# A transformer layer on one core: a new order of stores, bias additions, transposes and feed-forward turns

## The chip, the cores and the metric

The kernel runs on one core of a Trainium2 chip. The metric is the device time of one execution, in microseconds. A core has five engines that run their own instruction streams and meet at semaphores: TensorE (PE, matrix products; PEld is its loading of weights), VectorE (DVE), ScalarE (ACT), GpSimd (POOL) and SyncE (SP), which here issues all DMAs. Products land in PSUM, everything else lies in SBUF.

## The reference

The input x has 16 batches of 1024 rows of 256 numbers. The layer is, cut to what matters:

```python
xn = layernorm(x)
Q, K, V = xn @ Wq.T + bq, xn @ Wk.T + bk, xn @ Wv.T + bv       # 16 heads of 16
Q, K = rope(Q), rope(K)
weights = softmax(where(causal, Q @ K.T / 4, -1e9))
attn = (weights @ V) @ Wo.T + bo
y = square(relu(xn @ W_fc.T)) @ W_proj.T                        # 256 -> 1024 -> 256
spikes = count over 5 steps of a leaky threshold driven by y    # a step function of y
out = x + attn + spikes / 5
```

As the spikes are a step function of y, the kernel computes y nearly exactly: every operand of the projections is split into a high and a low part (xT_hi and xT_lo, h_hi and h_lo, and the weights), and three products are summed for each.

## The kernel before

The work is a pipeline over batches. `interval(b, ...)` exists once for each engine and lays the attention of batch b beside the preparation of batch b + 1 (its transposes, projections, rotation and the feed-forward part). There are 17 of them: one ahead (b = -1, no attention), one for b = 0, a loop for b = 1 to 13, one for b = 14, and a last one (b = 15, with the second half of its own feed-forward part and no projection).

An interval has 18 steps of 5 places, written (step, place). The places 0, 1, 3 and 4 hold one score group each: scores of 2 heads for 512 queries in all, against one to two tiles of 128 keys, in one of two PSUM buffers (`scores`, L1353), which ScalarE turns into probs (`weigh`, L759). TensorE waits before a group until the exponential of the group two before it is done. Place 2 holds a run of products of probs with v (`weigh`, L1370) and, for the batch before, `output`. Everything else stands in tables that map a place to work, and each engine walks its own part of them in this order. So an instruction that waits holds back all that stands behind it on its engine. GpSimd masks the tiles on the diagonal (L665), and the runs of products wait for these masks.

The parts that the change touches:

- Transposes of xn (`T_AT`, L1133) at place 2 of steps 2 and 3, split by ScalarE (`high_xT`, L716) and VectorE (`low_xT`, L865).
- Projection and rotation of four units u = 0 to 3 (`QK_AT`, L1153; `rotate`, L884 to L891): VectorE writes rot (eo = 0) and rot_b (eo = 1). GpSimd adds them (`sum_qk`, L647), ScalarE takes the high part into planes (`plane_qk`, L722), VectorE writes the low part over rot_b (`low_qk`, L895), and SyncE stores both to qk_dram (`store_planes`, L424). There are two buffers of each, so unit u waits for what unit u - 2 left: the second half of rotate, for the landing of its store (`planes_out[u % 2]`). The next projection waits for the rotation (`rot_done`), and so does the first expansion.
- The ring: SyncE reads q and k of a quad of heads (four in a batch) back into one of two slots with 13 DMAs (`load_ring`, L433 and L436), once the scores of the quad two before are done.
- The feed-forward part is cut in turns of 24 products (`MLP_AT`, L1175 and L1184). An item of it takes ScalarE's relu, VectorE's square and cast, and GpSimd's difference h_lo (L657). `Y_AT` is where VectorE takes a finished y.
- `add_bias` (L642) adds the output bias to rs, the residual rows, on GpSimd.

In the lines that stand below, `att` says that there is attention, `last` that there is a batch before it, `more` that there is one after.

## Time and profile before

| | us |
|---|---|
| median of 3 runs | 2242.65 (2242.55 to 2243.33) |
| the profiled execution | 2242.55 |
| its span, first to last instruction | 2240.8 |
| busy: TensorE | 2128.1 (95%) |
| busy: ScalarE | 1454.4 (65%) |
| busy: VectorE | 1385.8 (62%) |
| busy: GpSimd | 1112.1 (50%) |
| mean granted clock of TensorE | 0.988 |

The page gives for each group of instructions its busy time, the mean of one, and what ended the idle time before it. TensorE's share is above all others. In the 40 slices of the span it is at nine tenths or more in all but the first three and the last one, and the granted clock is at nine tenths or more in all but the second and the last. 46.6% of the time of the 16 DMA engines is taken by SyncE's queue. The timeline gives the start, length and idle time before each instruction, in us from the span's start.

### The profile page before, as it was taken

The page shows a single profiled execution, that of the slowest core. Times are in us where ns is not written, and L with a number is a line of the kernel's source. Part 1 is how long each engine was busy: PE and PEld are TensorE (multiplying, and loading weights), DVE is VectorE, ACT ScalarE, POOL GpSimd, SP SyncE. Part 2 cuts the span into 40 slices and gives each one's busy share as a digit, 9 for nine tenths or more (in the row PEclk, how much of TensorE's full clock was granted, in tenths as well). Part 3 has the DMA queues.
Part 4 walks back from the last instruction along what each step waited for, and adds up shares of the span by engine and source line. Part 5 has one row for each costly group of instructions (what it writes and reads, how often), then busy time and mean ns, then how long its engine had stood idle before and what let it go on. Part 6 is the DMA issues. An engine that isn't in the chain of part 4 may idle for free.

```text
span 2240.8 us, 67671 instructions
## 1 busy us (share of the span) xinstructions
PE 2128.1 (95%) x25492; PEld 1516.1 (68%) x25492; DVE 1385.8 (62%) x2134; ACT 1454.4 (65%) x1673; POOL 1112.1 (50%) x1074
## 2 busy tenths in 40 slices
PE   3789999999999999999999999999999999999995
PEld 2657677676767767676776767677676776767653
DVE  5555565675767657566665756667575666757543
ACT  2276766667676666767666676666767666676662
POOL 3445454463645547354553735455364544646341
PEclk9899999999999999999999999999999999999998
DMA  3354453535455363544536455453644535364442
GB/s 122 111 157 112 129 162 93 181 107 167 117 134 168 88 196 102 155 133 118 180 88 189 117 139 150 104 180 99 179 114 136 162 94 183 108 167 118 115 111 69
DMA packets 169850, 299.97 MB, mean 134 GB/s; under 512 B 25088, under 2 KB 114944, under 8 KB 157184
## 3 DMA queue, kind: packets, MB, share of 16 engines
q1 hardware_dynamic: 169600, 296.10, 46.6%
q8 instruction: 222, 3.64, 0.7%
q14 instruction: 28, 0.23, 0.0%
HBM read 174.89 MB, written 103.28 MB: 124 GB/s over the span
## 4 chain that ended last, share of the span: by engine, by line
PE 74%; DMA 6%; issue 6%; POOL 5%; DVE 4%; ACT 2%; SPq 0%; POOLq 0%; DVEq 0%; ACTq 0%
PE pair L1175 20%; PE pair L1370 18%; PE pair L1353 11%; PE pair L1184 10%; PE pair L1153 7%; PE pair L1115 6%; DMA recip_rows<-recip_dram 5%; POOL probs L665 3%; PE pair L1167 2%; ACT probs L759 2%; POOL h_lo L657 1%; POOL rs L642 1%; DMA recip_dram<-denom 1%; PE pair L1308 1%; DVE rot_b L891 1%
## 5 line engine op out<-in xcount | busy, mean ns | idle before, releaser
L759 ACT ACTIVATE probs<-pair 128x1024 f32<-128x1024 f32 x1152 | 1149.7, 1027 | 457.5 <-PE pair L1353 456.2
L657 POOL TENSOR_TENSOR h_lo<-h_sq,h_hi 128x512 fp32r<-128x512 f32 x256 | 386.7, 1510 | 467.7 <-DVE h_hi L963 467.4
L1184 PE MATMUL pair<-wproj_hi,h_hi 64*128 64x256 f32 x2048 | 599.1, 293 | 0.1
L1175 PE MATMUL pair<-xT_hi,wfc_hi 64*128 64x256 f32 x2048 | 556.2, 291 | 20.3 <-POOL h_lo L657 6.8
L1184 PE MATMUL pair<-wproj_hi,h_lo 64*128 64x256 f32 x2048 | 572.9, 280 | 0.0
L1184 PE MATMUL pair<-wproj_lo,h_hi 64*128 64x256 f32 x2048 | 572.1, 279 | 0.0
L665 POOL TENSOR_SCALAR_AFFINE_SELECT probs<-probs 128x512 f32<-128x512 f32 x512 | 386.4, 772 | 367.4 <-ACT probs L759 366.5
L1370 PE MATMUL pair<-probs,v_sb 128*17 128x512 f32 (+3 forms) x6144 | 549.9, 489 | 7.5 <-POOL probs L665 6.6
L1175 PE MATMUL pair<-xT_lo,wfc_hi 64*128 64x256 f32 x2048 | 536.8, 280 | 0.0
L1175 PE MATMUL pair<-xT_hi,wfc_lo 64*128 64x256 f32 x2048 | 536.0, 280 | 0.0
L1353 PE MATMUL pair<-q_ring,k_ring 64*128 64x512 f32 (+3 forms) x3072 | 463.3, 355 | 14.0 <-ACT probs L759 12.8
L1175 PEld LDWEIGHTS pair<-xT_hi,wfc_hi 64*128 64x128 f32 x2048 | 358.0, 187 | 72.2 <-PE pair L1175 31.4
L1184 PEld LDWEIGHTS pair<-wproj_lo,h_hi 64*128 64x128 f32 x2048 | 383.5, 187 | 1.8
L1184 PEld LDWEIGHTS pair<-wproj_hi,h_lo 64*128 64x128 f32 x2048 | 383.2, 187 | 0.0
L1184 PEld LDWEIGHTS pair<-wproj_hi,h_hi 64*128 64x128 f32 x2048 | 381.6, 186 | 0.9 <-issue 0.3
L961 DVE TENSOR_TENSOR h_sq<-h_sq 128x512 f32<-128x512 f32 x256 | 196.2, 766 | 292.7 <-ACT h_sq L751 289.5
L1353 PEld LDWEIGHTS pair<-q_ring,k_ring 64*128 64x128 f32 x3072 | 263.1, 186 | 160.7 <-ACT probs L759 89.0
L1175 PEld LDWEIGHTS pair<-xT_hi,wfc_lo 64*128 64x128 f32 x2048 | 359.5, 188 | 3.1
L1175 PEld LDWEIGHTS pair<-xT_lo,wfc_hi 64*128 64x128 f32 x2048 | 359.5, 188 | 0.0
L1370 PEld LDWEIGHTS pair<-probs,v_sb 128*17 128x17 f32 x6144 | 151.0, 97 | 281.6 <-issue 236.9
L751 ACT ACTIVATE h_sq<-pair 128x512 f32<-128x512 f32 x256 | 153.5, 600 | 179.5 <-PE pair L1175 101.1
L975 DVE SCALAR_TENSOR_TENSOR count<-y_sb,count 128x512 bf16<-128x512 f32 x256 | 261.5, 1022 | 4.2
(89 smaller groups left out, 2907.0 us busy)
## 6 DMA issues: line engine op xcount, KB each, us to landing
q_ring<-qk_dram SPq DMA_DIRECT2D x384, 128.0 KB
k_ring<-qk_dram SPq DMA_DIRECT2D x384, 128.0 KB
qk_dram<-planes SPq DMA_DIRECT2D x64, 512.0 KB, 2.8
qk_dram<-rot_b SPq DMA_DIRECT2D x64, 512.0 KB, 3.7
xn<-in_x SPq DMA_DIRECT2D x17, 1024.0 KB, 5.6
rs<-in_x SPq DMA_DIRECT2D x64, 256.0 KB, 2.8
acc_dram<-rs SPq DMA_DIRECT2D x64, 256.0 KB, 4.9
attn<-numer SPq DMA_DIRECT2D x256, 64.0 KB, 2.3
```

The source lines that it names most:

```text
L657: pool.tensor_tensor(h_lo[i % HB][:, :], h_sq[i % HB][:, :], h_hi[i % HB][:, :].bitcast(F32), ALU.subtract).then_inc(h_lo_done, 1)
L665: ins = pool.affine_select(view, view, [[0, 4], [1, P]], ALU.is_ge, 0.0, base=0, channel_multiplier=-1)
L751: act.activation(h_sq[i % HB][:, :], fc_bank[i % 2], ACT.Relu).then_inc(relu_done, 1)
L759: act.activation(probs[BUFFER[n]][:, 2 * pr:2 * pr + 2, :], pair[m % NSLOT][:, :, :], ACT.Exp, scale=SCALE).then_inc(exp_done, 1)
L961: dve.tensor_tensor(sq, sq, sq, ALU.mult).then_inc(sq_h, 1)
L975: dve.scalar_tensor_tensor(count[:, :], y, edges[s], count[:, :], ALU.is_gt, ALU.add).then_inc(spike_step, 1)
L1115: ins = pe.matmul(bank, lhsT, rhs, start=n == 0, stop=n == len(parts) - 1)
L1153: ins = pe.matmul(qk_bank[eo], w[rows, k, m], x[rows, k, cols], start=turn == 0 and n == 0, stop=turn == 1 and n == len(terms) - 1, skip_g ...
L1175: return pe.matmul(fc_bank[i % 2][:, a * T2:(a + 1) * T2], w[rows, k, m], x[rows, k, g * T2:(g + 1) * T2], start=turn == 0 and n == 0, sto ...
L1184: return pe.matmul(proj_bank[:, t * D:(t + 1) * D], h[rows, a * T2 + t * P:a * T2 + (t + 1) * P], w[rows, f, :], start=i % ITEMS_OF_GROUP ...
L1353: ins = pe.matmul(pair[m % NSLOT][:, half, to:to + width(kt, g)], k_ring[rows, slot, pr, kt * P:(kt + 1) * P], q_ring[rows, slot, pr, q0:( ...
L1370: ins = pe.matmul(pv_bank[32 * i:32 * i + VW, q0 - g * G:G], v_sb[:, kt, 4 * quad + i, :], probs[BUFFER[n]][:, i, at:at + width(kt, g)], s ...
```

## The change

It moves work and changes nothing of what is computed.

- SyncE: in the step 5 part, the load of the third quad's ring stands first, then for each unit the store of out and then that of the planes. Before, the planes stood ahead of out, and the ring behind the second of both.
- VectorE: `low_qk(u)` leaves the middle of the rotation of unit u + 1 and stands at place 3 of steps 4, 5 and 6; `low_xT` stands behind the copies of numer and the division.
- ScalarE: `plane_qk` is one place later, `high_xT` at place 2 and not 0.
- TensorE: the transposes stand behind the run of products; turns 2 to 16 and 22 to 24 of the feed-forward part stand at other places (most a place or two later).
- GpSimd: the four bias additions of a half stand together, at (2, 4) and at (13, 4). Before, they stood in pairs at (8, 2), (10, 2), (14, 2) and (15, 4).

```diff
--- before.py
+++ after.py
@@ -116,9 +116,9 @@
          (5, 4): (3, 0), (6, 0): (3, 1)}
 ROTATE_AT = {at: u for at, (u, turn) in QK_AT.items() if turn}
 SUM_QK_AT = {(3, 2): 0, (4, 2): 1, (5, 2): 2, (6, 2): 3}
-PLANE_AT = {(3, 4): 0, (4, 4): 1, (5, 4): 2, (6, 4): 3}
+PLANE_AT = {(4, 0): 0, (5, 0): 1, (6, 0): 2, (7, 0): 3}
 SQUARE_AT = {(4, 2): 0, (5, 2): 1, (6, 2): 2, (7, 2): 3}
-LOW_QK_AT = {(7, 2): 3}
+LOW_QK_AT = {(4, 3): 0, (5, 3): 1, (6, 3): 2, (7, 2): 3}
 O_AT = {4: 0, 5: 1, 6: 2, 7: 3}
 NORM_AT = 8
 NORM_PAIR = 4 * NORM_AT + 2
@@ -126,10 +126,10 @@
 
 
 
-MLP_AT = {(6, 4): (0,), (7, 0): (1,), (7, 4): (2,), (8, 0): (3,), (8, 2): (4, 5), (8, 4): (6,), (9, 0): (7,),
...
+MLP_AT = {(6, 4): (0,), (7, 0): (1,), (8, 0): (2,), (8, 2): (3, 4), (9, 0): (5,), (9, 3): (6,), (9, 4): (7,),
...
@@ -137,7 +137,7 @@
...
-Y_AT, Y_FIRST = {(10, 0): 0, (13, 0): 1, (16, 0): 2}, {(10, 1): 0, (13, 0): 1}
+Y_AT, Y_FIRST = {(10, 1): 0, (13, 0): 1, (16, 0): 2}, {(10, 1): 0, (13, 0): 1}
 Y_FINAL = {(11, 3): 2, (15, 3): 3}
 Y_CARRIED_AT = (1, 0)
...
@@ -182,7 +182,7 @@
 SPIKES_NEXT = {(14, 1): (0, 0), (14, 2): (0, 1), (14, 3): (0, 2), (14, 4): (0, 3), (15, 1): (0, 4), (15, 2): (0, 5),
                (15, 3): (1, 0), (15, 4): (1, 1), (16, 1): (1, 2), (16, 2): (1, 3), (16, 3): (1, 4), (17, 1): (1, 5)}
 SPIKES_FINAL = {(16, 0): 0, (17, 0): 1}
-BIAS_HERE_AT, BIAS_NEXT_AT = {(8, 2): (0,), (10, 2): (1,)}, {(14, 2): (0,), (15, 4): (1,)}
+BIAS_HERE_AT, BIAS_NEXT_AT = (2, 4), (13, 4)
 STATS_AT = {(10, 3): range(0, 4), (11, 4): range(4, 8)}
 VAR_AT, ROOT_AT = (11, 4), (12, 0)
 XN_AT, XN_FIRST = {(16, 4): range(0, 4), (17, 4): range(4, 8)}, {(13, 4): range(NT)}
@@ -530,12 +530,12 @@
                         load_ring(b, d, 1, b * 2 * NUNIT if last else None)
                     if last and n == 3:
                         load_fin(b - 1, d - 1, again)
+                    if att and n == 5:
+                        load_ring(b, d, 2, b * 2 * NUNIT + 2 * NU)
+                    if last and n in (5, 6, 7, 8):
+                        store_out(b - 1, d - 1, n - 5)
                     if more and n in (5, 6, 7, 8):
                         store_planes(nb, nd, n - 5)
-                    if last and n in (5, 6, 7, 8):
-                        store_out(b - 1, d - 1, n - 5)
-                    if att and n == 6:
-                        load_ring(b, d, 2, b * 2 * NUNIT + 2 * NU)
                     if att and n == 8:
                         gather(b, 0, last)
                     if norm and n == 8:
@@ -683,12 +683,14 @@
                         sum_qk(nb, SUM_QK_AT[at])
                     for i in expanded.get(at, ()) if more or final else ():
                         h_low(item, i)
-                    for a in BIAS_HERE_AT.get(at, ()) if att else ():
-                        add_bias(b, 1, a, again)
-                    for a in BIAS_NEXT_AT.get(at, ()) if more else ():
-                        if first and a == 0:
+                    if att and at == BIAS_HERE_AT:
+                        for a in range(2):
+                            add_bias(b, 1, a, again)
+                    if more and at == BIAS_NEXT_AT:
+                        if first:
                             pool.wait_ge(bias_done, 1)
-                        add_bias(nb, 0, a, again)
+                        for a in range(2):
+                            add_bias(nb, 0, a, again)
 
             root(0)
             low_weight(2)
@@ -776,7 +778,7 @@
                         weigh(b, 2 * n + place // 3, place % 3, last)
                     for m in take_v_at.get(at, ()) if att else ():
                         take_v(b, m)
-                    for m in T_AT.get(n, ()) if place == 0 and (more or final) else ():
+                    for m in T_AT.get(n, ()) if place == 2 and (more or final) else ():
                         high_xT(tb, m)
                     if more and at in PLANE_AT:
                         plane_qk(nb, PLANE_AT[at])
@@ -1010,23 +1012,20 @@
                         take_y(item + (y_at[at] + 1) * ITEMS_OF_GROUP, y_at[at])
                     if last and at == (0, 2):
                         take_numer(b - 1, *NUMER_AT[n], last)
-                    for m in T_AT.get(n, ()) if place == 2 and (more or final) else ():
-                        low_xT(tb, m)
                     if att and n and place == 2 and n in NUMER_AT:
                         take_numer(b, *NUMER_AT[n], last)
                     if last and at == INVERT_LAST:
                         invert(b - 1, 1)
                     if last and at == DIVIDE_LAST:
                         divide(b - 1, 1)
+                    for m in T_AT.get(n, ()) if place == 2 and (more or final) else ():
+                        low_xT(tb, m)
                     if more and at in ROTATE_AT:
-                        u = ROTATE_AT[at]
-                        if first and u == 0:
+                        if first and ROTATE_AT[at] == 0:
                             dve.wait_ge(table_in, 16)
                             dve.wait_ge(consts_done, 2)
-                        rotate(nb, u, 0, items_before(b, again) if att else None)
-                        if u:
-                            low_qk(nb, u - 1)
-                        rotate(nb, u, 1, None)
+                        for eo in range(2):
+                            rotate(nb, ROTATE_AT[at], eo, items_before(b, again) if att else None)
                     if last and place == 2 and n in O_AT:
                         finish(b - 1, O_AT[n])
                     if more and at in LOW_QK_AT:
@@ -1387,8 +1386,6 @@
                     n, place = at
                     if att and place != 2:
                         scores(b, 2 * n + place // 3, place % 3, last, more)
-                    for m in T_AT.get(n, ()) if place == 2 and (more or final) else ():
-                        transpose(b, tb, m, att, again)
                     if last and at == (0, 2):
                         run(b - 1, LAST_RUN, last)
                     if att and place == 2 and n in RUN_AT:
@@ -1397,6 +1394,8 @@
                         if att:
                             pe.wait_ge(exp_done, b * 2 * NUNIT + NORM_PAIR - NSLOT + 1)
                         norms(nb, first_norm_bank if first else norm_bank)
+                    for m in T_AT.get(n, ()) if place == 2 and (more or final) else ():
+                        transpose(b, tb, m, att, again)
                     if last and place == 2 and n in O_AT:
                         output(b - 1, O_AT[n])
                     if att and at in values_at:
```

SyncE in the loop, around the stores of unit 0 and the third ring (L424 is `store_planes`, L481 `store_out`, L433 and L436 `load_ring`). Before, from the store of rot_b of unit 0 to the first instruction of the ring load:

```order
L424 DMA qk_dram<-rot_b 128x2x512
L362 REGISTER_ALU
L481 DMA out<-fin 128x2x256
L362 REGISTER_ALU
L424 ISA
L424 DMA qk_dram<-planes 128x2x512
L424 ISA
L424 DMA qk_dram<-rot_b 128x2x512
L362 REGISTER_ALU
L481 DMA out<-fin 128x2x256
L362 REGISTER_ALU
L433 ISA
```

and now, from the last DMAs of the same ring load to the store of rot_b of unit 0:

```order
L433 DMA k_ring<-qk_dram 16x2048 x3
L436 ISA
L436 DMA q_ring<-shift_dram 2x2048
L362 REGISTER_ALU
L481 DMA out<-fin 128x2x256
L362 ISA
L424 ISA
L424 DMA qk_dram<-planes 128x2x512
L424 ISA
L424 DMA qk_dram<-rot_b 128x2x512
```

The 13 ring DMAs (q_ring, k_ring) moved from behind the second unit's stores to before those of the first, and out is ahead of the planes.

TensorE behind the last `output` (L1115, now L1114) in step 7, up to the first products of turn 2; the rows with q_ring are score groups. Before:

```order
L1115 MATMUL pair<-wo_sb,attn 128x256 x4
L1346 REGISTER_ALU
L1353 MATMUL pair<-q_ring,k_ring 128x512 x2
L1346 REGISTER_ALU
L1353 MATMUL pair<-q_ring,k_ring 128x512 x2
L1218 REGISTER_ALU
L1175 MATMUL pair<-xT_hi,wfc_hi 128x256
L1184 MATMUL pair<-wproj_hi,h_hi_53 128x256
```

and now:

```order
L1114 MATMUL pair<-wo_sb,attn 128x256 x4
L1345 REGISTER_ALU
L1352 MATMUL pair<-q_ring,k_ring 128x512 x2
L1345 REGISTER_ALU
L1352 MATMUL pair<-q_ring,k_ring 128x512 x2
L1345 REGISTER_ALU
L1352 MATMUL pair<-q_ring,k_ring 128x512 x2
L1217 REGISTER_ALU
L1174 MATMUL pair<-xT_hi,wfc_hi 128x256
L1183 MATMUL pair<-wproj_hi,h_hi_53 128x256
```

The group of (8, 0) has come before turn 2, so three groups follow one another.

GpSimd in steps 13 and 14, with h_lo of item 10 first (h_lo_59), the bias additions (rs) and the masks (probs). Before:

```order
L657 TENSOR_TENSOR h_lo_59<-h_sq_51,h_hi_55 128x512
L362 ISA
L665 AFFINE_SELECT probs<-probs 128x4x128 x2
L640 ISA
L642 TENSOR_TENSOR rs<-rs,bo_sb 128x256 x2
L656 REGISTER_ALU
L657 TENSOR_TENSOR h_lo_60<-h_sq_52,h_hi_56 128x512
L362 ISA
L665 AFFINE_SELECT probs<-probs 128x4x128 x2
```

and now:

```order
L657 TENSOR_TENSOR h_lo_59<-h_sq_51,h_hi_55 128x512
L640 ISA
L642 TENSOR_TENSOR rs<-rs,bo_sb 128x256 x4
L362 ISA
L665 AFFINE_SELECT probs<-probs 128x4x128 x2
L656 REGISTER_ALU
L657 TENSOR_TENSOR h_lo_60<-h_sq_52,h_hi_56 128x512
L362 ISA
L665 AFFINE_SELECT probs<-probs 128x4x128 x2
```

Four bias additions stand now before the masks of unit 28 and, behind h_lo of item 11, of unit 29; before there were two, between these masks.

## Rows read from the trace of the kernel before

**Rows 1.** Windows: one pass; columns in its heading.

```profile
core 0: us, PE busy (x) PEld busy (x) DVE busy (x) ACT busy (x) POOL busy (x), PEclk, DMA share, GB/s
1163.80:1296.20 132.40, 130.88 (x1596) 93.39 (x1594) 85.45 (x131) 90.33 (x105) 68.62 (x66) 1.00 0.48 138
```

**Rows 2.** Timeline (start, us, engine, line, out<-in, [idle before <-releaser]) of VectorE, numer.

```profile
1105.95 0.68 DVE L998 COPY numer<-pair 128x512 f32<-128x512 f32 x1
...
1238.36 0.68 DVE L998 COPY numer<-pair 128x512 f32<-128x512 f32 x1
```

**Rows 3.** Timeline of SyncE's queue, steps 4 to 6 of a pass.

```profile
1196.10 0.39 SPq L424 DMA_DIRECT2D qk_dram<-rot_b  x1
...
1205.80 0.65 SPq L481 DMA_DIRECT2D out<-fin  x1
...
1206.78 3.86 SPq L433 DMA_DIRECT2D q_ring<-qk_dram  x6
...
1216.30 0.38 SPq L424 DMA_DIRECT2D qk_dram<-rot_b  x1
```

**Rows 4.** Timeline of TensorE, the same steps.

```profile
1192.54 0.40 PE L1353 MATMUL pair<-q_ring,k_ring 64*128 64x512 f32 x2
...
1205.44 0.40 PE L1153 MATMUL pair<-xT_hi,wqk_hi 64*128 64x512 f32 x2
...
1213.63 0.28 PE L1175 MATMUL pair<-xT_hi,wfc_hi 64*128 64x256 f32 x2
...
1215.05 0.40 PE L1353 MATMUL pair<-q_ring,k_ring 64*128 64x384 f32 x4
```

**Rows 5.** Answer on the tile rot_b, one pass: issue to landing.

```profile
DMA to landing us min/median/max: 3.6/3.7/4.9
```

**Rows 6.** Timeline of VectorE, rotation of unit 2 in step 5.

```profile
1201.86 1.21 DVE L895 TENSOR_TENSOR rot_b<-rot,planes 128x1024 fp32r<-128x1024 f32 x1
1202.99 0.74 DVE L890 SCALAR_TENSOR_TENSOR rot_b<-pair,neg_bqk,table 128x512 f32<-128x512 f32 x1
```

**Rows 7.** Windows: two stretches of the last batch's attention.

```profile
2137.40:2140.80 3.40, 2.04 (x18) 1.03 (x20) 0.69 (x1) 2.59 (x3) 0.49 (x1) 1.00 0.70 198
2140.80:2144.20 3.40, 3.40 (x17) 0.50 (x9) 0.00 (x0) 1.18 (x2) 2.20 (x5) 0.50 0.24 82
```

**Rows 8.** Timeline of TensorE: a run of products at either clock.

```profile
1186.42 1.91 PE L1370 MATMUL pair<-probs,v_sb 128*17 128x512 f32 x16
...
2140.63 3.53 PE L1370 MATMUL pair<-probs,v_sb 128*17 128x512 f32 x16
```

**Rows 9.** Timeline of TensorE, steps 2 and 3 of a pass.

```profile
1179.39 2.35 PE L1370 MATMUL pair<-probs,v_sb 128*17 128x512 f32 x32
...
1189.36 0.50 PE L1153 MATMUL pair<-xT_hi,wqk_hi 64*128 64x512 f32 x2 [0.37 <-DVE rot_b L891]
```

**Rows 10.** Timeline of TensorE: score groups of the last stretch.

```profile
2146.05 0.73 PE L1353 MATMUL pair<-q_ring,k_ring 64*128 64x512 f32 x4
2147.72 0.49 PE L1353 MATMUL pair<-q_ring,k_ring 64*128 64x512 f32 x2 [0.94 <-ACT probs L759]
```

**Rows 11.** Timeline of GpSimd, steps 3 and 14.

```profile
1189.39 2.40 POOL L647 TENSOR_TENSOR rot<-rot,rot_b 128x1024 f32<-128x1024 f32 x1 [3.85 <-DVE rot_b L891]
...
1271.78 1.40 POOL L665 TENSOR_SCALAR_AFFINE_SELECT probs<-probs 128x512 f32<-128x512 f32 x2
...
1273.16 1.87 POOL L642 TENSOR_TENSOR rs<-rs,bo_sb 128x256 f32<-128x256 f32 x2
...
1276.12 1.67 POOL L657 TENSOR_TENSOR h_lo<-h_sq,h_hi 128x512 fp32r<-128x512 f32 x1 [1.09 <-DVE h_hi L963]
...
1277.75 2.12 POOL L665 TENSOR_SCALAR_AFFINE_SELECT probs<-probs 128x512 f32<-128x512 f32 x2
```

**Rows 12.** Timeline of TensorE, the run in step 15.

```profile
1277.58 1.92 PE L1370 MATMUL pair<-probs,v_sb 128*17 128x512 f32 x24
...
1279.92 0.63 PE L1370 MATMUL pair<-probs,v_sb 128*17 128x256 f32 x8 [0.42 <-POOL probs L665]
```

**Rows 13.** Waits, first 150 us: us in total, times, longest us.

```profile
PE pair L1153 <- DVE rot_b L891: 12.2, 5, 4.0
```

6 rows, old and new, of the table MLP_AT are left out of this document.

## The prediction

> **What bounds the kernel now.** I read the windows first. The reader is to see one pass of the batch loop in them: 132.40 us long, TensorE busy for 130.88 of it (98.9%), no other engine above 71% (VectorE 85.45, ScalarE 90.33, GpSimd 68.62), and the granted clock 1.00 [rows 1]. The pass repeats exactly: the same copy into numer stands at 1105.95 and at 1238.36 [rows 2]. So TensorE bounds the pass, 1.5 us of it are idle, and no order of the work can give back more than that. There are 16 batches. The 15 stretches in which one batch's attention runs beside the next batch's preparation (b = 0 to 14) use the tables that change; the first stretch (no attention) and the last (own tables) hardly do. So there is hardly any slack to win, and each new wait of TensorE is paid 15 times. I therefore went through the timelines engine by engine and asked of each moved instruction who is made late.
>
> Places are written (step, place), as in the tables; one step is two score units.
>
> **The change part by part.**
>
> *SyncE: the third ring load goes ahead of the store of the planes.* Before, rot_b of unit 0 is sent at 1196.10, and the 13 ring DMAs start only at 1206.78, after out (1205.80) [rows 3]. Now the ring stands first. Its wait is for the scores of the first quad, that is for place (4, 1), at 1192.54 + 0.40 [rows 4]. So it starts at 1192.94 + 0.25 (TensorE late by then, below) + 0.15 to leave the wait = 1193.3. From the start of a ring load to the rot_b that follows it directly before (1206.78 to 1216.30) are 9.5 us; the store of out now stands between, and from out to the next DMA are 0.98 us (1205.80 to 1206.78) [rows 3]. rot_b of unit 0 is then sent at 1193.3 + 9.5 + 1.0 = 1203.8, 7.7 us later than at 1196.10. Landing takes 3.6, 3.7 or 4.9 us [rows 5]; the longest is the one right behind a ring load, and so is this one: 1208.7.
>
> Who waits for that: VectorE's second half of the rotation of unit 2 overwrites rot_b 0 and waits for planes_out[0]. It ran at 1202.99 [rows 6]. Now it starts at 1208.7 and its two operations of 0.74 us, overlapped, end 1.4 us on, at 1210.1. Behind it in VectorE's order stand a copy of numer, finish and the low part of unit 1; TensorE waits for it in front of the projection of unit 3, which stood at 1205.44 [rows 4]. It resumes 1210.1 - 1205.44 = **4.65 us** late; I take 4.6. With a landing of 3.6 it is 3.35. Taking the low part (1201.86 to 1202.99, 1.13 us) out of the rotation helps nothing here, as the DMA comes last [rows 6].
>
> The same wait stands in unit 3's rotation. From 1210.1 on, numer, finish and low part take 2.5 us, sending 0.7, landing 3.7, the two operations 1.4: 8.3. TensorE needs 1213.63 - 1205.44 = 8.2 from there to the first expansion [rows 4], which waits for it. The second wait is thus covered by the first; if this landing took 4.9 as well, 1.2 more.
>
> On that landing the Trainium skill (DMA: Bandwidth & Descriptors, section "Queues, rings and completion order") says that each DMA engine takes descriptors in ring order, but that a later DMA of an issuing engine need not complete after an earlier one. By the first half the store pays for the ring's tail (4.9, the term above), by the second it might land as on an empty queue (3.6, a term of 3.35). The trace has 4.9 behind a ring, so I go by that.
>
> *The clock.* In the last stretch TensorE was busy 2.04 of 3.40 us, waiting for ScalarE, and in the following 3.40 us the granted clock was 0.50, the lower of its two levels (1.2 GHz) [rows 7]; a run of products x16 took 3.53 us there and 1.91 at 1.00 [rows 8]. A wait of 4.6 us leaves TensorE idler than that. If one such stretch follows each, it does 3.40 x 1.91 / 3.53 = 1.84 us of work: **1.5 us** lost. Bounds: 0, and two stretches, 3.0.
>
> *Transposes behind the run (2, 2).* The run (1179.39, 2.35 us) now precedes them [rows 9], so xT_hi and xT_lo come later, at most by 2.3, and the first projection waits some 0.8 us by my estimate. But the next projection already waits 0.37 us for rot_b [rows 9], and the rotation before it is tied to a division that waits for a DMA. Bounds 0 and 2.3; I take 0.25, contained in the term above. The transposes of (3, 2) are wanted first by (4, 2) and cost nothing, nor does ScalarE's xT_hi behind one more exponential.
>
> *The turns of the feed-forward part.* Turn 2 leaves (7, 4) for (8, 0), and (8, 4) loses its turn. Score groups (7, 3), (7, 4), (8, 0), and again (8, 3), (8, 4), (9, 0), now stand with nothing between. Each group needs the exponential of the group two before it. The last stretch shows that pattern: groups at 2146.05, and the third at 2147.72 after 0.94 us idle on ScalarE [rows 10]. Twice 0.94 is 1.9, less 0.2 for the wait for finish at (7, 4) that goes: **1.7 us** (0.9 to 2.4, if restarts cost 0.25 each more). The remaining turns to (12, 4) move by a place with at least 0.5 us for h_lo by my count, and Y_AT follows them.
>
> *GpSimd: both bias additions at (13, 4).* These are four operations, two of which take 1.87 [rows 11]. After h_lo of item 10 GpSimd is free at 1271.78. Then come 2 x 1.87 = 3.74 of bias (before, the mask of unit 28 and one pair lay there), the mask of unit 28 at 1.40, h_lo 1.67, and the mask of unit 29, at 1.40 too: 1279.99. Before, TensorE waited 0.42 for that mask and went on at 1279.92 [rows 12]. Now it reaches the run one turn earlier and goes on at 1280.1, 0.2 later, but with turn 23 still to do: 1215.05 - 1213.63 = 1.42 us and about 0.3 for the change to it [rows 4]. Together **1.9 us**. Cover gone: any delay of POOL here is TensorE's. If both masks stretch to 2.12, as one did, it is 3.3; at the least the turn's 1.42 stays. The other pair, at (2, 4), lies in the 3.85 us in which GpSimd sits idle before rot [rows 11], and fits (3.74); what it may push, the planes of unit 0, is behind the ring anyway.
>
> On the stretching, the Trainium skill (SBUF — State Buffer, "Who interferes with whom") says a GpSimd operation that reads SBUF and a VectorE operation with two SBUF inputs exclude each other. By it the four additions meet VectorE's spike counts and the term goes to 3.3. The row has 1.87 for a pair beside the same counts, and I keep that.
>
> *First stretch.* There TensorE waits for rot_b five times, 12.2 us [rows 13]; three rotations lose the 1.13 us of the low part from their middle: -3.4 (0 at worst, if the late planes take it back).
>
> **Sum.** 4.6 + 1.5 + 1.7 + 1.9 = 9.7 us per stretch, x 15 = 145.5; less 3.4: +142. The profiled execution took 2242.55 (span 2240.8 and 1.75 around it; the median is 2242.65): 2384.7, **2385 us**.
>
> **Rivals.**
> - *The clock does not fall* (idle in places too short or cut in two): 8.2 x 15 - 3.4 = +120, 2362. For it: 22 of the 142 us rest on a pattern seen in one place. Against: TensorE was less idle there than it will be in a wait of 4.6 us.
> - *The ring is hidden*: the transfers overlap or SyncE starts it earlier, so only turns, masks and 0.25 stay: 3.85 x 15 - 3.4 = +54, 2297. Against: 7.7 us later against a spare of 3.2 (landed at 1196.10 + 3.7 = 1199.8, used at 1202.99).
> - *Only the ring costs*, masks and scores fit: 6.1 x 15 - 3.4 = +88, 2331.
> - *Faster*: the low part leaves the rotation, so rot_done comes 1.13 us earlier in three places, and GpSimd is free at (8, 2) and (10, 2). If planes landed before 1202, TensorE would lose its idle time of 1.5 us: -22.5 - 3.4 = -26, 2217. It decides if the store lands before 1202.99, within 9.7 us of the ring's start; [rows 3, 5] put the landing at 15.4 (9.5 + 1.0 + 4.9), so I give it little.
> - *The change doesn't do what it says*: terms cancel or the schedule had more play than a modelled end shows; 2243.
>
> **How the numbers follow.** Forecast 0.57 (own range 2350 to 2425), no fall of the clock 0.15, only the ring 0.10, ring hidden 0.09, faster 0.05, cancelled 0.04. The range 2315 to 2425 leaves out the ring hidden, both last ones and a little above (clock falling twice, second wait uncovered): about 2 in 10. 0.2% (4.5 us) is what the measurement tells from no change: slower 0.91, same 0.04, faster 0.05.
>
> **What would show it.** A pass of about 142 us. TensorE idle some 4 to 5 us before the projection of unit 3 (released by rot_b), with VectorE idle before its second half of rotation of unit 2, released by the DMA from rot_b; a clock of 0.5 behind it; TensorE idle about 0.9 us on ScalarE at (8, 0) and (9, 0); and about 2 us on the mask in the last run of step 15. SyncE's ring DMAs stand before the first store of the planes. Wrong if VectorE isn't found waiting there, if the clock stays 1.00, or if the pass stays under 136 us.

## The result and the profile after

The kernel after takes 2439.39 us (median of 4 runs, 2433.15 to 2440.19), the kernel before 2242.60 us in the runs beside it (2240.86 to 2243.33): a ratio of 1.0873, 95% interval 1.0854 to 1.0892. It is slower by 197 us. The profiled execution took 2436.61 us, with a span of 2434.8. The forecast was 2385 with a range of 2315 to 2425: right in direction, wrong in size, and the time lies outside the range.

Some line numbers shift by one or two: scores are L1352, products with v L1369, projections L1152, expansions L1174, rotate L886 to L893, low part L897, the exponential L761. The first thing to read is a pass, as in [rows 1]. The first window covers two passes, the second all 13 passes of the loop, from one first projection of a pass to another; columns are window, length, busy time (and instructions) of PE, PEld, DVE, ACT, POOL, granted clock, DMA share, GB/s. Under them stand stretches of 3.40 us around two waits.

```profile
995.10:1286.14 291.04, 269.82 (x3194) 192.22 (x3192) 177.51 (x263) 181.99 (x209) 139.14 (x135) 0.97 0.44 126
...
263.35:2158.35 1895.00, 1752.18 (x20698) 1248.79 (x20698) 1153.77 (x1703) 1181.35 (x1353) 898.49 (x858) 0.97 0.44 126
...
1242.60:1246.00 3.40, 1.16 (x16) 0.70 (x18) 2.12 (x3) 0.07 (x1) 2.19 (x3) 1.00 0.59 183
1246.00:1249.40 3.40, 3.40 (x36) 3.31 (x34) 1.31 (x3) 2.07 (x3) 0.00 (x0) 0.50 0.62 193
...
1307.50:1310.90 3.40, 0.00 (x0) 0.00 (x0) 0.62 (x1) 1.06 (x2) 0.00 (x0) 1.00 0.11 40
1310.90:1314.30 3.40, 2.56 (x12) 2.07 (x14) 3.40 (x5) 0.00 (x0) 2.53 (x2) 0.50 0.11 36
1314.30:1317.70 3.40, 3.40 (x18) 2.24 (x16) 0.93 (x1) 1.97 (x2) 2.01 (x2) 0.50 0.52 190
1317.70:1321.10 3.40, 3.40 (x38) 1.67 (x37) 2.80 (x5) 1.97 (x2) 0.00 (x0) 1.00 0.42 159
```

A pass takes 291.04 / 2 = 145.5 us instead of 132.40, and 13.1 x 15 = 197 us: the size of the whole loss, which lies in the 15 stretches that the prediction named. (Over the 13 passes of the loop the mean is 145.8 us instead of 132.5, of which 9.4 us are waits and 3.9 busy time; the passes differ by up to 2.2 us.) TensorE is busy 134.9 us a pass instead of 130.88 and idle 10.6 instead of 1.5. So 9.1 us of the 13.1 are waits. The other 4.0 are busy time for the same products, and the windows show how: behind the wait that ends at 1244.84 stand 3.40 us at a clock of 0.50, and around the end of the wait at 1311.74 6.8 us. The records of the granted clock between 250 and 2200 us have one such stretch of 3.4 us before and 27 with 122.9 us in all after. That is 9.2 us a pass at half clock, in which 4.0 us were lost, some 0.44 of each. The passes bear it out: the nine of the loop with 10.2 us at half clock took 145.5 to 146.9 us, the four with 6.8 us 144.6 to 145.1.

The waits by name, of the whole span (us in total, times, longest), TensorE's and one of VectorE:

```profile
PE pair L1152 <- DVE rot_b L893: 79.6, 18, 6.4
PE pair L1352 <- ACT probs L761: 41.8, 48, 1.7
PE pair L1369 <- POOL probs L665: 41.1, 17, 2.7
...
PE pair L1152 <- DVE xT_lo L867: 16.8, 16, 1.5
...
PE pair L1174 <- DVE y_sb L992: 5.3, 15, 0.8
...
DVE rot_b L892 <- DMA qk_dram<-rot_b: 121.5, 31, 7.8
```

In the same view of before the first four stood at 18.0, 12.8, 6.6 and 1.5 us, and the last, VectorE waiting for a store, was not there at all. It is there 31 times, twice a pass.

TensorE in one pass, at the four places where it now waits (answering to [rows 4, 9, 10, 12]); the number in brackets is the idle time ahead of the row:

```profile
1244.84 0.63 PE L1369 MATMUL pair<-probs,v_sb 128*17 128x256 f32 x8 [2.69 <-POOL probs L665]
...
1283.89 0.50 PE L1152 MATMUL pair<-xT_hi,wqk_hi 64*128 64x512 f32 x2 [1.02 <-DVE xT_lo L867]
...
1311.74 0.79 PE L1152 MATMUL pair<-xT_hi,wqk_hi 64*128 64x512 f32 x2 [4.93 <-DVE rot_b L893]
...
1331.63 0.50 PE L1352 MATMUL pair<-q_ring,k_ring 64*128 64x512 f32 x2 [0.89 <-ACT probs L761]
...
1340.91 0.51 PE L1352 MATMUL pair<-q_ring,k_ring 64*128 64x512 f32 x2 [0.89 <-ACT probs L761]
```

2.69 + 1.02 + 4.93 + 2 x 0.89 and 5.3 / 15 for y_sb are 10.8 us, about the 10.6 that were idle per pass of the first window. (The step-5 wait is not the same in every pass: 3.5 to 5.6 us, 4.7 on average of 14.) SyncE's queue in steps 4 to 6 (answering to [rows 3]):

```profile
1294.41 3.85 SPq L433 DMA_DIRECT2D q_ring<-qk_dram  x6
1298.44 3.80 SPq L433 DMA_DIRECT2D k_ring<-qk_dram  x6
1302.42 0.52 SPq L436 DMA_DIRECT2D q_ring<-shift_dram  x1
1303.17 0.41 SPq L481 DMA_DIRECT2D out<-fin  x1
1304.03 0.40 SPq L424 DMA_DIRECT2D qk_dram<-planes  x1
1304.61 0.37 SPq L424 DMA_DIRECT2D qk_dram<-rot_b  x1
```

And VectorE beside it (answering to [rows 6]):

```profile
1298.58 1.64 DVE L897 TENSOR_TENSOR rot_b<-rot,planes 128x1024 fp32r<-128x1024 f32 x1
...
1310.28 0.75 DVE L892 SCALAR_TENSOR_TENSOR rot_b<-pair,neg_bqk,table 128x512 f32<-128x512 f32 x1 [7.12 <-DMA qk_dram<-rot_b]
...
1312.80 2.43 DVE L897 TENSOR_TENSOR rot_b<-rot,planes 128x1024 fp32r<-128x1024 f32 x1
...
1319.71 0.75 DVE L892 SCALAR_TENSOR_TENSOR rot_b<-pair,neg_bqk,table 128x512 f32<-128x512 f32 x1 [0.60 <-DMA qk_dram<-rot_b]
```

The chain of the step-5 wait can be followed row by row: the ring's 13 DMAs start at 1294.41, rot_b 0 is sent at 1304.61 behind them, its landing releases VectorE at 1310.28 after 7.12 us, and TensorE's projection follows at 1311.74. The low part, no longer inside the rotation, was done at 1300.2, 4.4 us before its buffer's store was even sent.

GpSimd ahead of the mask that TensorE waits for in step 15 (answering to [rows 11]):

```profile
1235.77 3.45 POOL L642 TENSOR_TENSOR rs<-rs,bo_sb 128x256 f32<-128x256 f32 x4
1239.17 1.86 POOL L665 TENSOR_SCALAR_AFFINE_SELECT probs<-probs 128x512 f32<-128x512 f32 x2
1241.01 1.70 POOL L657 TENSOR_TENSOR h_lo<-h_sq,h_hi 128x512 fp32r<-128x512 f32 x1
1242.66 2.13 POOL L665 TENSOR_SCALAR_AFFINE_SELECT probs<-probs 128x512 f32<-128x512 f32 x2
```

The order is the one predicted. The four additions took 3.45 instead of the 3.74 booked, both masks more than the 1.40 booked, and from the first addition to the end of the second mask it is 9.0 us instead of 8.2.

### The profile page after: what moved, and what is told of

Read it like the earlier page. It is cut to its first block and busy times, and to the rows that moved or that the text cites. A ratio compares the mean times of both kernels' runs of the same rounds, so it can differ in the third digit from the quotient of the medians.

```text
span 2434.8 us, 67671 instructions
## 1 busy us (share of the span) xinstructions
PE 2184.2 (90%) x25492; PEld 1553.9 (64%) x25492; DVE 1431.1 (59%) x2134; ACT 1462.3 (60%) x1673; POOL 1122.6 (46%) x1074
## 5 line engine op out<-in xcount | busy, mean ns | idle before, releaser
L761 ACT ACTIVATE probs<-pair 128x1024 f32<-128x1024 f32 x1152 | 1148.0, 1027 | 645.3 <-PE pair L1352 645.0
L1369 PE MATMUL pair<-probs,v_sb 128*17 128x512 f32 (+3 forms) x6144 | 556.9, 492 | 43.5 <-POOL probs L665 41.1
L665 POOL TENSOR_SCALAR_AFFINE_SELECT probs<-probs 128x512 f32<-128x512 f32 x512 | 417.6, 833 | 358.8 <-ACT probs L761 358.7
L1174 PE MATMUL pair<-xT_hi,wfc_hi 64*128 64x256 f32 x2048 | 563.1, 294 | 16.0 <-DVE y_sb L992 5.3
L1174 PE MATMUL pair<-xT_lo,wfc_hi 64*128 64x256 f32 x2048 | 545.3, 285 | 0.0
L1174 PE MATMUL pair<-xT_hi,wfc_lo 64*128 64x256 f32 x2048 | 544.6, 284 | 0.0
L1352 PE MATMUL pair<-q_ring,k_ring 64*128 64x512 f32 (+3 forms) x3072 | 473.0, 360 | 41.9 <-ACT probs L761 41.8
L1174 PEld LDWEIGHTS pair<-xT_hi,wfc_hi 64*128 64x128 f32 x2048 | 368.5, 192 | 56.5 <-issue 17.7
L1183 PEld LDWEIGHTS pair<-wproj_lo,h_hi 64*128 64x128 f32 x2048 | 392.1, 191 | 2.3
L1183 PEld LDWEIGHTS pair<-wproj_hi,h_hi 64*128 64x128 f32 x2048 | 390.8, 191 | 0.9 <-issue 0.3
L1352 PEld LDWEIGHTS pair<-q_ring,k_ring 64*128 64x128 f32 x3072 | 265.4, 190 | 186.7 <-ACT probs L761 111.3
L1174 PEld LDWEIGHTS pair<-xT_hi,wfc_lo 64*128 64x128 f32 x2048 | 369.3, 193 | 5.1
L1174 PEld LDWEIGHTS pair<-xT_lo,wfc_hi 64*128 64x128 f32 x2048 | 368.4, 192 | 0.0
L1369 PEld LDWEIGHTS pair<-probs,v_sb 128*17 128x17 f32 x6144 | 149.7, 97 | 329.1 <-issue 229.4
L977 DVE SCALAR_TENSOR_TENSOR count<-y_sb,count 128x512 bf16<-128x512 f32 x256 | 293.7, 1147 | 4.7
L647 POOL TENSOR_TENSOR rot<-rot,rot_b 128x1024 f32<-128x1024 f32 x64 | 156.4, 2444 | 262.8 <-DVE rot_b L893 262.7
```

The source lines that it names most:

```text
L647: pool.tensor_tensor(rot[u % 2][:, :, :], rot[u % 2][:, :, :], rot_b[u % 2][:, :, :], ALU.add).then_inc(rot_sum, 1)
L665: ins = pool.affine_select(view, view, [[0, 4], [1, P]], ALU.is_ge, 0.0, base=0, channel_multiplier=-1)
L761: act.activation(probs[BUFFER[n]][:, 2 * pr:2 * pr + 2, :], pair[m % NSLOT][:, :, :], ACT.Exp, scale=SCALE).then_inc(exp_done, 1)
L977: dve.scalar_tensor_tensor(count[:, :], y, edges[s], count[:, :], ALU.is_gt, ALU.add).then_inc(spike_step, 1)
L1174: return pe.matmul(fc_bank[i % 2][:, a * T2:(a + 1) * T2], w[rows, k, m], x[rows, k, g * T2:(g + 1) * T2], start=turn == 0 and n == 0, sto ...
L1183: return pe.matmul(proj_bank[:, t * D:(t + 1) * D], h[rows, a * T2 + t * P:a * T2 + (t + 1) * P], w[rows, f, :], start=i % ITEMS_OF_GROUP ...
```

## The experiments

Theory A is the prediction's: ring ahead of the store, turns and mask each cost TensorE a wait. What it left open is the clock. Theory B is that each of the two larger waits (step 5 and the mask in step 15) brings more time at half clock than was booked, and that this is the missing part. "Per pass" is the difference of the medians divided by 15.

### The parts one by one

**Only SyncE's order** (e1). In `interval`, on the kernel before:

```diff
+                    if att and n == 5:
+                        load_ring(b, d, 2, b * 2 * NUNIT + 2 * NU)
+                    if last and n in (5, 6, 7, 8):
+                        store_out(b - 1, d - 1, n - 5)
                     if more and n in (5, 6, 7, 8):
                         store_planes(nb, nd, n - 5)
-                    if last and n in (5, 6, 7, 8):
-                        store_out(b - 1, d - 1, n - 5)
-                    if att and n == 6:
-                        load_ring(b, d, 2, b * 2 * NUNIT + 2 * NU)
```

> The kernel before with SyncE's new order alone (the third ring load ahead of the stores, out ahead of the planes). Theory (each moved part costs by its own wait, and the granted clock falls behind a wait of several us): TensorE waits 4.5 to 5 us a pass for rot_b in front of the projection of unit 3, the clock falls for one or two stretches of 3.41 us behind it, 1.5 to 2.4 us more; together about 6.5 us x 15 = 98 us, 2340 us (2325 to 2355). Rival 1 (the ring is hidden when nothing else is moved): under 2260. Rival 2 (the parts add up only together, since the late low part of unit 0 delays the store as much as the ring does): 2290 or less.

Measured: 2347.33 (2346.57 to 2349.80) against 2240.13, ratio 1.0479 (1.0462 to 1.0497), +7.1 us a pass. TensorE at the projection of unit 3, and then the waits:

```profile
1267.54 0.80 PE L1153 MATMUL pair<-xT_hi,wqk_hi 64*128 64x512 f32 x2 [5.92 <-DVE rot_b L891]
```

```profile
PE pair L1153 <- DVE rot_b L891: 89.9, 31, 5.9
```

and the windows around it:

```profile
1261.50:1264.90 3.40, 0.12 (x3) 0.00 (x0) 0.00 (x0) 1.86 (x2) 0.00 (x0) 1.00 0.71 264
1264.90:1271.70 6.80, 4.16 (x20) 3.14 (x22) 2.60 (x4) 1.62 (x2) 3.55 (x3) 0.51 0.30 108
```

This part alone makes the wait, and the half clock behind it is twice the stretch that the prediction booked: 92.2 us between 250 and 2200 us, in 14 falls. Of the 7.1 us a pass the wait for rot_b gives (89.9 - 18.0) / 15 = 4.8. The slow products give 2.2: TensorE is busy for 2160.9 us of the span instead of 2128.1. That is less than 0.44 of the time at half clock, which began before the wait had ended, so that TensorE was busy for only 4.16 of the 6.80 us above. The edit moves two things, the ring and the store of out ahead of the planes; out takes 0.9 us of the queue (1303.17 to 1304.03 in the kernel after) and was not tried apart.

**Only the bias additions** (e2). The edit is that of the change to `BIAS_HERE_AT`, `BIAS_NEXT_AT` and GpSimd's loop:

```diff
-BIAS_HERE_AT, BIAS_NEXT_AT = {(8, 2): (0,), (10, 2): (1,)}, {(14, 2): (0,), (15, 4): (1,)}
+BIAS_HERE_AT, BIAS_NEXT_AT = (2, 4), (13, 4)
```

> The kernel before with the four bias additions together at (2, 4) and (13, 4) alone. Prediction's reading (GpSimd's additions make the masks of unit 29 late): TensorE reaches the run of step 15 as before, waits for the mask until about 1280.0 instead of 1279.5, so 0.1 to 0.5 us x 15: 2244 to 2250. Rival (the additions alone cost the 1.9 us that the prediction booked under them, or more with a fall of the clock): 2271 to 2295.

Measured: 2258.98 (2256.12 to 2263.59) against 2240.13, ratio 1.0077 (1.0060 to 1.0094), +1.25 a pass, more than expected. The wait for the mask went from 6.6 to 22.8 us, 1.1 a pass:

```profile
PE pair L1372 <- POOL probs L665: 22.8, 15, 1.8
```

The clock fell at two places only (6.8 us). So the additions alone cost 1.25. The 1.9 that stood under their name was made of 0.2 for a later mask and 1.7 for the turn that now stands behind the run.

**Only the feed-forward turns** (e3): the change's `MLP_AT` and `Y_AT`.

```diff
-MLP_AT = {(6, 4): (0,), (7, 0): (1,), (7, 4): (2,), (8, 0): (3,), (8, 2): (4, 5), (8, 4): (6,), (9, 0): (7,),
+MLP_AT = {(6, 4): (0,), (7, 0): (1,), (8, 0): (2,), (8, 2): (3, 4), (9, 0): (5,), (9, 3): (6,), (9, 4): (7,),
...
-Y_AT, Y_FIRST = {(10, 0): 0, (13, 0): 1, (16, 0): 2}, {(10, 1): 0, (13, 0): 1}
+Y_AT, Y_FIRST = {(10, 1): 0, (13, 0): 1, (16, 0): 2}, {(10, 1): 0, (13, 0): 1}
```

> The kernel before with the new table of feed-forward turns alone (and the place of the first y copy that goes with it). Theory: three score groups in a row at (8, 0) and (9, 0), 0.9 us each; the run of step 15 comes one turn earlier and meets the mask of unit 29 at its old time (1279.9), so it waits about 2.2 us more, and the clock falls behind that wait for one stretch (1.5 us): 1.8 + 1.8 + 1.5 = 5.1 us x 15 = 77 us, 2320 us. Rival (without the additions in front of the masks the run finds them done): 1.8 x 15, 2270 us.

Measured: 2300.75 (2297.87 to 2301.46) against 2240.13, ratio 1.0269 (1.0252 to 1.0286), +4.0 a pass, below the expected 2320. The wait for ScalarE at the scores rose from 12.8 to 40.2 us (1.8 a pass, as forecast) and, without any addition moved, the wait for the mask from 6.6 to 31.0 (1.6 a pass), with 37.5 us at half clock in 11 falls. The mask wait in step 15 thus belongs more to the turns than to the additions. (One of the 11 falls stands behind another wait; 10 of the 14 mask waits in that stretch have one.)

**Only turns 22 to 24** (e9), to tell that apart:

```diff
-          (14, 0): (20,), (14, 3): (21,), (14, 4): (22,), (15, 0): (23,), (15, 3): (24,),
+          (14, 0): (20,), (14, 3): (21,), (15, 0): (22,), (15, 3): (23,), (15, 4): (24,),
```

> The kernel before with turns 22 to 24 alone at their new places ((15, 0), (15, 3), (15, 4)). Theory: no third score group in a row and no late addition, only the run of step 15 one turn early against the mask of unit 29: 1.6 to 1.7 us a pass and a fall of the clock in most passes (37.5 us at half clock in 14 passes of the full table, so 1.2 more): 2.4 to 2.9 x 15, 2279 to 2286 us. Rival (the full table's clock falls come from the score groups): 1.6 x 15, 2266 or less, clock 1.00.

Measured: 2277.05 (2273.43 to 2279.27) against 2241.43, ratio 1.0153 (1.0132 to 1.0174), +2.4 a pass, just below the expected 2279. The wait at the scores stayed at 12.8, the one for the mask was that of e3:

```profile
PE pair L1370 <- POOL probs L665: 31.1, 15, 2.2
```

Windows around one of them:

```profile
1292.90:1296.30 3.40, 1.34 (x26) 0.38 (x18) 2.25 (x2) 0.16 (x1) 2.78 (x3) 1.00 0.45 123
1296.30:1299.70 3.40, 3.40 (x32) 3.31 (x30) 1.29 (x2) 1.10 (x2) 0.00 (x0) 0.51 0.64 190
```

Behind a wait of 2.06 us, with TensorE busy 1.34 of 3.40 us ahead of the fall, there is a stretch at 0.51. The prediction had looked for a fall only behind its wait of 4.6 us. The same wait did not bring one every time, and that gives the price of a fall inside one execution. Of the 13 passes of the loop seven have one stretch of 3.4 us at half clock and take 134.9 to 136.4 us (mean 135.7), six have none and take 134.0 to 134.1. Two neighbours, a pass with the stretch and one without:

```profile
1333.68:1469.32 135.64, 132.40 (x1598) 94.97 (x1594) 85.72 (x132) 90.29 (x105) 68.23 (x67) 0.99 0.47 135
1469.32:1603.42 134.10, 130.88 (x1598) 93.46 (x1594) 86.23 (x132) 90.30 (x105) 68.68 (x67) 1.00 0.48 137
```

TensorE is busy 1.5 us longer for the same products: the price per stretch that the prediction had booked. Why the clock fell in one pass and not in the next is not known.

**Turns and additions together** (e10), the edits of e3 and e2:

```diff
+MLP_AT = {(6, 4): (0,), (7, 0): (1,), (8, 0): (2,), (8, 2): (3, 4), (9, 0): (5,), (9, 3): (6,), (9, 4): (7,),
...
+BIAS_HERE_AT, BIAS_NEXT_AT = (2, 4), (13, 4)
```

> The kernel before with the new turns and the four bias additions together. Theory (parts add, as the additions delay the same mask that the turns reach early: 4.0 + 1.25 us a pass): 2242 + 60.6 + 18.8 = 2321 us (2312 to 2330). Rival (the two waits for one mask overlap, the larger counts): 2303.

Measured: 2319.22 (2313.42 to 2336.74) against 2241.43, ratio 1.0361 (1.0308 to 1.0414), +5.2 a pass. Turns and additions alone add up to 60.6 + 18.9 = 79.5 us, together they cost 77.8: they add, as nearly as these runs can tell. The mask wait is 41.1, exactly that of the full change.

**Only the transposes** (e6), moved behind the run on all three engines. TensorE's part of it:

```diff
-                    for m in T_AT.get(n, ()) if place == 2 and (more or final) else ():
-                        transpose(b, tb, m, att, again)
                     if last and at == (0, 2):
                         run(b - 1, LAST_RUN, last)
...
+                    for m in T_AT.get(n, ()) if place == 2 and (more or final) else ():
+                        transpose(b, tb, m, att, again)
```

> The kernel before with the transposes behind the run of products, and ScalarE's and VectorE's parts of them moved with them, alone. Prediction: 0.25 us a pass, 2244 us. Rival from the trace of the changed kernel (TensorE waits 1.05 us a pass for xT_lo, less the 0.37 that it waited for rot_b before): 0.7 to 1.0 us a pass, 2250 to 2256.

Measured: 2249.53 (2245.85 to 2252.42, 6 runs) against 2242.11, ratio 1.0034 (1.0022 to 1.0046), +0.5 a pass, between both cases. The waits show the exchange that the prediction described: xT_lo rises from 1.5 to 16.8, rot_b falls from 18.0 to 12.2.

```profile
PE pair L1153 <- DVE xT_lo L865: 16.8, 16, 1.5
...
PE pair L1153 <- DVE rot_b L891: 12.2, 5, 4.0
```

**Only the low part out of the rotation** (e7), with `PLANE_AT` a place later:

```diff
-PLANE_AT = {(3, 4): 0, (4, 4): 1, (5, 4): 2, (6, 4): 3}
+PLANE_AT = {(4, 0): 0, (5, 0): 1, (6, 0): 2, (7, 0): 3}
-LOW_QK_AT = {(7, 2): 3}
+LOW_QK_AT = {(4, 3): 0, (5, 3): 1, (6, 3): 2, (7, 2): 3}
...
-                        rotate(nb, u, 0, items_before(b, again) if att else None)
-                        if u:
-                            low_qk(nb, u - 1)
-                        rotate(nb, u, 1, None)
+                        for eo in range(2):
+                            rotate(nb, ROTATE_AT[at], eo, items_before(b, again) if att else None)
```

> The kernel before with low_qk out of the rotation and plane_qk one place later, alone. Prediction: nothing in a pass, as the late store hid it, and 3.4 us gained in the first stretch: 2237 us. Rival (the low part now comes behind numer and finish, so the store of unit 1 and with it the second half of unit 3's rotation are late, and the first expansion waits): about 1 us a pass, 2250 to 2258. If the shorter rotation helped in each pass: 2225 or less.

Measured: 2267.02 (2259.70 to 2273.76, 6 runs) against 2242.11, ratio 1.0108 (1.0090 to 1.0127), +1.66 a pass. Both cases missed it. VectorE in steps 5 and 6:

```profile
1216.77 0.75 DVE L890 SCALAR_TENSOR_TENSOR rot_b<-pair,neg_bqk,table 128x512 f32<-128x512 f32 x1 [1.56 <-DMA qk_dram<-rot_b]
...
1219.29 2.45 DVE L895 TENSOR_TENSOR rot_b<-rot,planes 128x1024 fp32r<-128x1024 f32 x1
...
1226.27 0.75 DVE L890 SCALAR_TENSOR_TENSOR rot_b<-pair,neg_bqk,table 128x512 f32<-128x512 f32 x1 [2.87 <-DMA qk_dram<-rot_b]
```

and the waits:

```profile
PE pair L1172 <- DVE rot_b L891: 16.6, 16, 3.1
...
PE pair L1350 <- ACT probs L759: 17.9, 25, 1.7
...
DVE rot_b L890 <- DMA qk_dram<-rot_b: 68.5, 31, 3.1
```

The low part of unit 1 runs after the copy of numer and finish, and takes 2.45 us there instead of 1.21 [rows 6]. Only then is its store sent, and the rotation two units on waits for it to land: VectorE waits 68.5 us for it, where it had waited for none, and TensorE is late at the first expansion (16.6 us, 5.7 before) and at the scores (17.9, 12.8 before). This is a wait on the same semaphore as the ring's, by another way, and the prediction did not have it. These waits make 16 of the 25 us. The rest is busy time of TensorE, 131.4 us a pass instead of 130.9 at a granted clock of 1.00 in both; e4 has the same, and what makes it was not looked for. So up to 0.5 of the 4.0 us of busy time in the full change may be something other than the clock.

**The ring one step earlier, but behind the store** (e12):

```diff
-                    if att and n == 6:
+                    if att and n == 5:
```

> The kernel before with the third ring load moved by one: behind the stores of unit 0, ahead of nothing else than the stores of unit 1 on. Theory (what costs is the store that a rotation waits for, not the transfers of the ring): unit 0's store is as before, unit 1's comes 4 to 5 us later and lands 1 to 2 us after unit 3's rotation wants it; 1.0 of that is spare: 0 to 1.2 us a pass, 2242 to 2260, no wait for unit 2. Rival (the ring's transfers beside the stores cost by themselves): over 2290.

Measured: 2246.17 (2241.09 to 2248.94, 10 runs) against 2241.43 (13 runs), ratio 1.0021 (1.0011 to 1.0031), +0.3 a pass. The same 13 transfers, in the same step as in e1, cost 0.3 us instead of 7.1 when rot_b 0 is sent ahead of them. VectorE waits 13.2 us in all for the store. So it is the place in the queue that costs, hardly the ring's traffic.

**The change without SyncE's part** (e4): the kernel after, with the old order of ring and stores.

```diff
-                    if att and n == 5:
-                        load_ring(b, d, 2, b * 2 * NUNIT + 2 * NU)
-                    if last and n in (5, 6, 7, 8):
-                        store_out(b - 1, d - 1, n - 5)
                     if more and n in (5, 6, 7, 8):
                         store_planes(nb, nd, n - 5)
+                    if last and n in (5, 6, 7, 8):
+                        store_out(b - 1, d - 1, n - 5)
+                    if att and n == 6:
+                        load_ring(b, d, 2, b * 2 * NUNIT + 2 * NU)
```

> The changed kernel with SyncE's old order alone. Theory: the wait for rot_b and its fall of the clock go, what is left is turns, masks, transposes and the fall of the clock behind the mask wait: 13.1 - 6.5 = 6.6 us x 15 = 99 us over before, 2342 us (2325 to 2360). Rival (the late low parts of the rotation keep the stores late and the wait with them): over 2380.

Measured: 2363.83 (2355.97 to 2372.71) against 2240.13, ratio 1.0563 (1.0538 to 1.0587), +8.2 a pass: above what was expected. Its waits:

```profile
PE pair L1352 <- ACT probs L761: 56.2, 60, 1.7
...
PE pair L1174 <- DVE rot_b L893: 16.5, 16, 3.2
```

The last line is e7's wait (16.6). The full change has 4.2 us of it, 3.6 of these in the first stretch: the wait behind the ring covers it. That is one reason why the parts alone add up to more than the whole: 107.2 + 60.6 + 18.9 + 7.4 + 24.9 = 219 us against 196.8. With the rest in place SyncE's order is worth 75 us, alone 107. The four other parts add up to 111.8 us alone and cost 123.7 here, so they don't just add either: at the scores TensorE waits 56.2 us here, where the 12.8 of before and what e3 (27.4) and e7 (5.1) add make 45.3.

### The clock by itself

These kernels repeat score products of place (5, 4), or also of (15, 1), in front of the wait. They write the same values again, so TensorE does more work and waits less. If only waits and work counted, no such kernel could be faster than the one that it fills.

**Only SyncE's order, wait filled** (e8):

```diff
-                for seg, (kt, g) in enumerate(UNITS[n % NU]):
+                for seg, (kt, g) in [x for _ in range(18 if m == 23 and bounded else 1) for x in enumerate(UNITS[n % NU])]:
```

> The kernel before with SyncE's new order and the same 17 extra score groups at (5, 4). Theory: the wait of about 4.9 us stays as time but the clock stays at 1.00: 2347 - 44 = 2303 us (2295 to 2320). Rival (clock without a part in it): 2347 or more.

Measured: 2321.07 (2320.48 to 2321.26) against 2242.11, ratio 1.0352 (1.0337 to 1.0367), just above the expected 2295 to 2320. That is 26 us less than e1, with more products to compute. The filling, the window around it, and VectorE, which still waits for the same store:

```profile
1245.71 4.82 PE L1353 MATMUL pair<-q_ring,k_ring 64*128 64x256 f32 x76
```

```profile
1243.00:1250.00 7.00, 7.00 (x90) 5.85 (x84) 1.78 (x3) 1.83 (x2) 1.99 (x2) 1.00 0.65 229
```

```profile
1249.14 0.75 DVE L890 SCALAR_TENSOR_TENSOR rot_b<-pair,neg_bqk,table 128x512 f32<-128x512 f32 x1 [5.22 <-DMA qk_dram<-rot_b]
```

The clock stays at 1.00, and between 250 and 2200 us there is no stretch at half clock (92.2 us in e1). The account closes. TensorE's wait for rot_b fell by 68.1 us (89.9 to 21.8), the filling is 65.0 us of products (2193.1 us busy instead of 2128.1), the 32.8 us of slow products of e1 are gone, and a new idle time came up ahead of the projection of v, for which the profile names nothing that TensorE waited for:

```profile
PE pair L1167 <- issue: 10.0, 12, 1.2
```

68.1 - 65.0 + 32.8 - 10.0 = 25.9 us. So the filling was about as long as the wait that it replaced, and the gain is what the clock gave back, less these 10 us.

**The change, step-5 wait filled** (e5): the same line in the kernel after.

```diff
+                for seg, (kt, g) in [x for _ in range(18 if m == 23 and bounded else 1) for x in enumerate(UNITS[n % NU])]:
```

> The changed kernel; the score products of place (5, 4) are done 18 times over instead of once (same result into the same buffer), so that TensorE works for about 4.6 us (17 x 0.27) where it sat idle before the projection of unit 3. Theory (the granted clock falls because of the idle time, and the fall costs about 2.9 us a pass beside the wait: 6.6 us at half clock, 0.44 lost of each): although TensorE does more work, 2385 to 2405 us. Rival (the clock costs nothing there or falls anyway): 2439 or more.

Measured: 2431.17 (2419.86 to 2431.83) against 2242.11, ratio 1.0828 (1.0806 to 1.0849): 8 us less than the change, not the 34 to 54 that were expected. Half clock fell from 122.9 to 47.8 us, worth 33 us by 0.44. The filling (65 us of products, by e8) took the place of 68.0 us of waiting for rot_b (79.6 to 11.6). But TensorE then waited 18.6 us for rot_b at the first expansion, 4.2 in the full change, and 9.6 us in the place that e8 shows, 24 us in all. The expectation had priced neither. By itself this run doesn't decide the matter.

**The change, both waits filled** (e11), with a shorter filling in step 5 (the expectation calls e5's filling 5.5 us long; by e8's 65.0 / 15 it is 4.3):

```diff
+                for seg, (kt, g) in [x for _ in range({23: 15, 61: 7}.get(m, 1) if bounded else 1) for x in enumerate(UNITS[n % NU])]:
```

> The changed kernel with both long waits of TensorE filled to a little less than their length: the score products of (5, 4) 15 times over and those of (15, 1) 7 times. At 18 times the filling was longer than the wait (5.5 us to 4.5, from the sync-only kernels: 83 us of products against 68 of wait). Theory: no stretch at half clock in the passes and no work longer than a wait: of 3.9 us a pass of clock loss 1.1 turns into the wait of the first expansion for unit 3, so 2.8 x 15 = 42 us less, 2397 us (2385 to 2410). Rival (the clock is a small part, its falls hide in waits): over 2425.

Measured: 2408.96 (2405.27 to 2415.10) against 2241.43, ratio 1.0741 (1.0720 to 1.0763): 30 us less than the change, with more work. Half clock is 10.2 us of the 122.9 that there were (112.7 x 0.44 = 50 us). Not all of that comes back, as the first expansion waits (20.9 us) and the idle time ahead of v (11.4 us) are new. What is left of the waits:

```profile
PE pair L1369 <- POOL probs L665: 25.2, 15, 1.9
PE pair L1174 <- DVE rot_b L893: 20.9, 16, 2.9
PE pair L1152 <- DVE rot_b L893: 18.7, 16, 3.2
```

With e8 and the passes of e9 this bears theory B out: a part of the loss is neither wait nor work but products at half clock.

## Why the prediction was wrong in size

The step that failed is **the clock**. The prediction booked "if one such stretch follows each, ... 1.5 us lost", for the step-5 wait alone, with bounds of 0 and 3.0. Measured are two falls a pass, 9.2 us at half clock and 3.9 to 4.0 us lost, above its upper bound. The price of a stretch was right (1.5 us, and e9 shows 1.5); their number was wrong, 2.7 stretches of 3.4 us a pass instead of one. The 27 falls last 6.83 us nine times, seven of them behind the step-5 wait, and 3.41 us eighteen times; 13 of the 27 stand behind the mask wait in step 15, for which nothing was booked. 2.4 us x 15 = 36 of the missing 54 us are this. Shown by the busy time of the pass, by e8 and e11, and by the passes of e9 with and without a fall. (Up to 0.5 us a pass of it may be the busy time that e7 and e4 add at full clock.) The rival that the clock doesn't fall (2362) is out.

The other steps, one by one:

- **Ring ahead of the store**: mechanism right in each link (e1, and e12 as the counter-proof). From the ring's start to rot_b sent 10.2 us (10.5 forecast), landing 1310.28 - 1304.61 = 5.7 instead of 4.9, restart 1.46 (1.4). TensorE's wait is 4.93 in this pass, of which 0.37 was there before: 4.6 more, and 4.3 more by the average wait of 4.7. A landing of 3.6 us, which the second half of the rule in the Trainium skill (DMA: Bandwidth & Descriptors, "Queues, rings and completion order") would have allowed, did not come: behind the ring the store took 5.7 us. Whether it was the ring's tail that it waited for, no run here shows.
- **Second wait covered**: right. VectorE waits 0.60 us at 1319.71, TensorE not at all in this pass.
- **Transposes**: 0.25 taken inside the step-5 term; the trace has 1.02 us on xT_lo, while the 0.37 on rot_b behind it goes; e6 measured 0.5. Within the bounds of 0 and 2.3, but a quarter of a microsecond or more too low.
- **Turns, three score groups in a row**: 0.94 forecast at each, 0.89 measured at each. Y_AT, which "follows them", costs 0.35 a pass (5.3 / 15), booked at nothing.
- **GpSimd and the mask**: 1.9 forecast, 2.69 - 0.42 = 2.27 measured. The sum was nearly right, its parts less so: it had 1.7 for the turn and 0.2 for a later mask. In waits for the mask, turns 22 to 24 alone cost 1.6 us a pass (e9), the additions alone 1.1 (e2), both together 2.3 (e10). The masks took 1.86 and 2.13 instead of 1.40. By the rule on GpSimd and VectorE in the Trainium skill (SBUF — State Buffer, "Who interferes with whom") the prediction had put the term at 3.3, with slower additions. The four additions took 3.45 instead of 3.74, so they weren't slower. VectorE beside them was: its square took 1.26 us (at 1238.51), and 0.69 in the kernel before (at 1268.40), with GpSimd idle. That fits the rule, with VectorE as the one that waits; no experiment tried it.
- **Low part out of the rotation**: "helps nothing here" was right in the full change, but the reason was incomplete. By itself it costs 1.66 a pass (e7), 1.1 of it in waits, because its store is sent later; the ring hides that. The forecast had no such mechanism.
- **First stretch, -3.4**: its waits fell as forecast, the time can't be told from scatter. In the first 100 us TensorE waits 11.6 us for rot_b instead of 15.0, and the first projection of the next stretch starts at 119.79 instead of 123.44. But in five other kernels that leave the first stretch as it was (e1, e3, e8, e9, e12) it starts at 120.7 to 124.4.

Together, by the 13 passes of the loop, the waits came to 9.4 us a pass instead of 8.2 (18 of the missing 54 us) and the clock to 3.9 instead of 1.5 (36). The split of the 4.93 us between the landing and what else was late was not tried apart.

No experiment pointed to an order faster than the kernel before: every part alone is slower than it, the smallest by 0.34% (and the ring a step earlier, behind the store, by 0.21%).
